# The shifted value copy of a two-layer local attention: fourteen ScalarE activations a batch replaced by DMAs from ScalarE's queue

## The chip, the cores and the metric

The kernel runs on one core of one Trainium2 chip. The metric is the device time of one execution in microseconds; the figure for a kernel is the median of its runs.

## The reference

The program takes 16 sequences ("batches") of 512 tokens with 128 features and runs two residual blocks on each. The first block multiplies a recurrent unit (a log-space gated recurrence, `gru` in the kernel) by a gate that comes from a two-layer transformer with local attention. The second multiplies a global attention (16 heads of 16, softmax over the queries, `glob` in the kernel) by a gate from a mixture of experts. The change lies in the local attention. Windows are of 64 tokens, and a token of window w attends to windows w-1 and w:

```python
bv = v.reshape(b, h, w, WINDOW, d)                 # WINDOW = 64, d = 64, h = 8
def look_around(t):
    p = jnp.pad(t, ((0, 0), (0, 0), (1, 0), (0, 0), (0, 0)))
    return jnp.concatenate([p[:, :, :w], p[:, :, 1:]], axis=3)
bk, bv = (look_around(bk), look_around(bv))
...
out = jnp.einsum('bhwij,bhwjd->bhwid', attn, bv)
```

So each query needs the value rows of its own window and of the one before.

## The kernel before

A batch's 512 tokens are worked on as NT = 4 tiles (t = 0 to 3) of 128 tokens, two windows each. The value rows of tile t lie in `va[:, t]`, tokens on partitions, 8 heads of 64 values and a column of ones (65 floats a head, 520 floats or 2080 bytes in a row for one partition). VectorE writes them out of PSUM (line 1200). The second window of a tile finds the window before it in the upper and lower half of that tile; the first window of a tile needs the last window of the tile before. For that there is a second tensor, `vb`: its lower 64 partitions at tile t hold the lower 64 of `va` at t, and its upper 64 partitions at t + 1 hold the upper 64 of `va` at t. ScalarE fills it, step `("vb", t)`: an activation from partitions 64 to 127 for t = 0, 1, 2 (line 944), and one from partitions 0 to 63 for all four t (line 945). That is 7 activations a layer, 14 a batch and 224 in the program. The reader of `vb` is step `("pv", 2t)` on TensorE (line 725, recorded under the matmul helper's line 587), which first waits for the mark "c" of `("vb", t)` (line 716).

The work of several batches runs at once. Each pass of the outer loop works on lanes: `p` (the projections of local attention: q, k, v, `vb`, the rotation `rot` and `rot2`, the turns `tq` and `tk`, for layer 1 of the batch before and layer 0 of this one), `q` (scores, softmax and its turn, `pturn`), `r` (`pv`, `oturn`, `wo`, and the layer's first feed-forward), `s` (input norm, recurrence, second feed-forward, gate), `g` (the global attention, mostly of two batches back) and `x` (the experts, which run once, in the last pass). The table `ORDER` is a string for each engine which says from which lane the next step comes; each engine issues its instructions in exactly that order, so an instruction that waits holds up everything behind it on its engine. Steps wait for each other by semaphores counted through the tables of marks (`QKV_MARKS` and its like): `need(engine, flow, producer, b, step, mark)` waits until the producer has passed that mark. All DMAs of before are issued from SyncE: the input (line 506), the parts of q and k of the global attention stored to HBM (line 516), their reload in pairs `qs`, `ks` (line 529), and the output (line 534).

Other names in the rows: `e` is the PSUM bank of the projections and of the turns `tq`, `tk` (PSUM out by ScalarE, lines 933 and 957); `scratch<-pb` on line 974 is `pturn` on ScalarE and on line 966 the exponentials of a tile's softmax; `ex` on line 1033 are the exponentials of the global attention, `nmax` on line 1307 their maxima on VectorE; `o_bank` are the global attention's products; lines 889 and 892 are steps of a norm, line 979 is `oturn`.

Of the kernel before, what the change touches and what calls it, by code (L numbers as in the profile page):

```python
# [27 lines left out]
ACT = mybir.ActivationFunctionType  # L28
X = mybir.AxisListType.X

P = 128
B, N, D = 16, 512, 128
NT = N // P
DIN = 256
JG = DIN // P
DEPTH, HEADS, DH, WIN = 2, 8, 64, 64
# [115 lines left out]
def expert_steps():  # L152
# [31 lines left out]
    "q": {"pe": ["p"], "act": ["c"]},  # L184
    "k": {"pe": ["p"], "act": ["c", "sq"]},
    "v": {"pe": ["p"], "dve": ["c"]},
    "vb": {"act": ["c"]},
    "rot": {"dve": ["ss", "max", "c", "s0", "s1"], "pool": ["add"], "act": ["ln", "inv"]},
    "rot2": {"dve": ["n1", "n2", "inv"], "pool": ["q"]},
    "tq": {"pe": ["t"], "act": ["t"]},  # L190
# [71 lines left out]
def lanes():  # L262
# [14 lines left out]


ORDER = {
    "pe": ("3xsgpsxgp8xg4x2gp2xsgxgp28xp4xps2gpspgpxspq3g4xgxpgxqsgqxpsgprpqsp3gpgrqrp3grqxrpgrqr2grpqg2xgxpqgrp"  # L280
           "gqgxprgqpr2gpsgrqprgp3g2r2pgrgpqp2gpqs2grqsgpgpgrpq2gspsgxqpsr2gsrgpqrsprgsgrq2gqgsgprqgpr3gqgrgs2gr"
           "gqsrgq3rsrsrsrgs3r3g4r15g"),
    "act": ("2xsp2gps2gsgp4x2pgs3pg3p2gpxs2g2s2qgqgpg2pqg2pqgp2gpsrg2qgpgq2ps2gxrqgp2qgpgqgspgqpgqrqgpg2pgp2gqp2g"
            "rps2pgpqp3g2qs2gqpspsp2g2pgsgqsgp2qpr2spq3gpgprg2q2gqpsgpsgq3gq2gsr2gq2s2x2qgr4s3r3srs3r17g"),
    "dve": ("xp4x2gs3g2p3x3g17x2s2psps2g2s3gqsgp2sp2gs3xgpxsqg2sr2g2p2grp2grsrgrpq2gsgrp2gr2gqgrspgxp2grgrg2p2gxr"
            "p3grqsgx2psgr2gpgsgsx2gq2gxr3pgrsgrsr3gpqs2g2s2grg2sgr3gqrgs3gr2x2s2rs2r2srsrsrg3s4r9g"),
    "pool": ("gpg2psgs2pgspgs2p2gpg2pgp2g3pgpgsgs3g"),
}


# [33 lines left out]
def need(eng, flow, producer, b, step, mark):  # L324

    if b < 0:
        return
    eng.wait_ge(flow.sem[producer], flow.count(producer, b, step, mark))


def build(nc, a, out):
    ctx = ExitStack()
    with ctx:
        ctx.enter_context(nc.allow_non_contiguous_dma(reason="bias columns, once, a few KB"))

        def sb(name, shape, dt=F32):
            return ctx.enter_context(nc.sbuf_tensor(name, shape, dt))
# [4 lines left out]
        def sem(name):  # L342
            return ctx.enter_context(nc.semaphore(name))
# [4 lines left out]
        qkv = flows["qkv0"], flows["qkv1"]  # L348
# [4 lines left out]
        parts_stored = [sem("parts_even_stored"), sem("parts_odd_stored")]  # L353
        stack_loaded = [sem("stack_even_loaded"), sem("stack_odd_loaded")]
        prep_pe, prep_dve, prep_act, prep_pool = (sem(f"prepared_by_{e}") for e in ("pe", "dve", "act", "pool"))
        expert_loaded = [sem(f"expert_loaded_{i}") for i in range(4)]


# [33 lines left out]
        va, vb = sb("va", [P, NT, HEADS, DH + 1]), sb("vb", [P, NT, HEADS, DH + 1])  # L392
# [192 lines left out]
        def _(pe):  # L585
            def mm(o, l, r, start=True, stop=True):
                return pe.matmul(o, l, r, start=start, stop=stop, skip_group_check=True)  # L587
# [120 lines left out]
            def head_does(l, b, s):  # L708
                f, kind = head[l], s[0]
                if kind == "pv":  # L710
                    u = s[1]
                    t, par = u // 2, u % 2
                    if par:
                        need(pe, f, "dve", b, ("pv", u - 1), "o")
                    else:
                        need(pe, qkv[l], "act", b, ("vb", t), "c")
                        if t:
                            need(pe, f, "dve", b, ("wo", t - 1), "x")
                        elif l == 0:
                            need(pe, head[1], "dve", b - 1, ("wo", NT - 1), "x")  # L720
                    need(pe, attn[l], "act", b, ("pturn", u), "t")
                    for r in range(PAIRS):
                        for w, v in ((0, vb), (1, va)):
                            last = mm(bank_c[WIN * w:WIN * w + WIN, (DH + 1) * r:(DH + 1) * (r + 1)],
                                      probT[u % 2][:, r, WIN * w:WIN * w + WIN], v[:, t, 2 * r + par, :])
                    last.then_inc(f.sem["pe"], 1)
                elif kind == "oturn":
                    t = s[1]
                    need(pe, f, "dve", b, ("pv", 2 * t + 1), "o")
                    for r in range(PAIRS):  # L730
                        last = pe.transpose(bank_c[:, P * r:P * r + P], o_row[:, P * r:P * r + P], ident)  # L731
                    last.then_inc(f.sem["pe"], 1)
                else:
                    t = s[1]
                    need(pe, f, "act", b, ("oturn", t), "t")
                    for r in range(PAIRS):
                        last = mm(bank_c[:, 0:P], wo[:, l, r, :], oT[:, r, :], start=(r == 0), stop=(r == PAIRS - 1))
                    last.then_inc(f.sem["pe"], 1)
# [88 lines left out]
            def expert_does(b, s):  # L827
# [31 lines left out]
                "qkv0": lambda b, s: qkv_does(0, b, s), "qkv1": lambda b, s: qkv_does(1, b, s),  # L859
                "attn0": lambda b, s: attn_does(0, b, s), "attn1": lambda b, s: attn_does(1, b, s),  # L860
                "head0": lambda b, s: head_does(0, b, s), "head1": lambda b, s: head_does(1, b, s),
                "post0": lambda b, s: post_does(0, b, s), "post1": lambda b, s: post_does(1, b, s), "expert": expert_does})


        @block.scalar
        def _(act):
            A = nc.scalar.activation
# [57 lines left out]
            def qkv_does(l, b, s):  # L925
                f, kind = qkv[l], s[0]
                FA = f.sem["act"]
                if kind in ("q", "k"):
                    t, k = s[1], int(kind == "k")
                    if t and kind == "q":  # L930
                        need(act, f, "dve", b, ("rot", t - 1), "s1")
                    need(act, f, "pe", b, s, "p")
                    A(l_qk[:, INNER * k:INNER * (k + 1)], bank_e, ACT.Copy).then_inc(FA, 1)  # L933
                    if k:
                        if t:
                            need(act, f, "pool", b, ("rot", t - 1), "add")
                        need(act, f, "act", b, s, "c")
                        A(l_sq, l_qk, ACT.Square).then_inc(FA, 1)
                elif kind == "vb":

                    t = s[1]
                    need(act, f, "dve", b, ("v", t), "c")
                    if t < NT - 1:
                        A(vb[WIN:P, t + 1, :, 0:DH], va[WIN:P, t, :, 0:DH], ACT.Copy)
                    A(vb[0:WIN, t, :, 0:DH], va[0:WIN, t, :, 0:DH], ACT.Copy).then_inc(FA, 1)
                elif kind == "rot":
                    need(act, f, "dve", b, s, "max")
                    A(stat[:, 16:32], stat[:, 0:16], ACT.Ln, scale=2.0 ** NORM_SHIFT).then_inc(FA, 1)
                    need(act, f, "act", b, s, "ln")
                    A(stat[:, 32:48], stat[:, 16:32], ACT.Exp, scale=-0.5, bias=norm_bias).then_inc(FA, 1)  # L950
                elif kind in ("tq", "tk"):
                    t = s[1]
                    dst = qT[:, :, P * t:P * t + P] if kind == "tq" else kT[:, :, WIN + P * t:WIN + P * t + P]
                    if kind == "tq" and l == 0:
                        need(act, attn[1], "pe", b - 1, ("score", min(t + 1, NT - 1)), "s")
                    need(act, f, "pe", b, s, "t")
                    A(dst, bank_e.rearrange("p (r n) -> p r n", r=PAIRS), ACT.Copy).then_inc(FA, 1)
# [87 lines left out]
            def expert_does(b, s):  # L1045
# [18 lines left out]
            run(act, "act", {  # L1064
                "pre": pre_does, "gru": gru_does, "glob": glob_does,
                "qkv0": lambda b, s: qkv_does(0, b, s), "qkv1": lambda b, s: qkv_does(1, b, s),
                "attn0": lambda b, s: attn_does(0, b, s), "attn1": lambda b, s: attn_does(1, b, s),
                "head0": lambda b, s: head_does(0, b, s), "head1": lambda b, s: head_does(1, b, s),
# [401 lines left out]
```

## Time and profile before

| | us |
|---|---|
| median of 3 runs (lowest, highest) | 3660.54 (3658.41, 3660.62) |
| the profiled execution, whole | 3663.09 |
| its span, first to last instruction | 3661.3 |
| granted TensorE clock, mean | 0.937 |

The span and every row are of the one profiled execution, which lies 2.55 us above the median. Engines are PE (TensorE matmuls), PEld (its weight loads), DVE (VectorE), ACT (ScalarE), POOL (GpSimd) and SP (SyncE). Instructions that wait or that issue a DMA belong to an engine's sequencer (SPq, ACTq) and count as no busy time. The chain of waits is followed back from the last instruction, at each step to what released it or else to the instruction ahead of it on its engine.

### The profile page before, as it was taken

The page shows a single profiled execution, that of the slowest core. Times are in us where ns is not written, and L with a number is a line of the kernel's source. Part 1 is how long each engine was busy: PE and PEld are TensorE (multiplying, and loading weights), DVE is VectorE, ACT ScalarE, POOL GpSimd, SP SyncE. Part 2 cuts the span into 40 slices and gives each one's busy share as a digit, 9 for nine tenths or more (in the row PEclk, how much of TensorE's full clock was granted, in tenths as well). Part 3 has the DMA queues.
Part 4 walks back from the last instruction along what each step waited for, and adds up shares of the span by engine and source line. Part 5 has one row for each costly group of instructions (what it writes and reads, how often), then busy time and mean ns, then how long its engine had stood idle before and what let it go on. Part 6 is the DMA issues. An engine that isn't in the chain of part 4 may idle for free.

```text
span 3661.3 us, 54935 instructions
## 1 busy us (share of the span) xinstructions
PE 3026.1 (83%) x20144; PEld 1454.9 (40%) x20144; DVE 2466.6 (67%) x4573; ACT 2551.7 (70%) x5722; POOL 922.2 (25%) x685
## 2 busy tenths in 40 slices
PE   4677897989888897979889897988889798988776
PEld 2343443434344343524344343534434343433242
DVE  3465867768685877768586776868586776857313
ACT  2466777868686777868677786868677786857444
POOL 1131323223131323313132322323132322312000
PEclk9889998999999999999999999999999998989887
DMA  2001010010101001010101001010101001011200
GB/s 71 3 1 51 18 51 17 14 58 19 58 14 51 21 31 41 14 58 18 54 18 51 21 25 47 14 58 19 54 18 47 21 14 55 19 51 36 83 9 16
DMA packets 113448, 122.78 MB, mean 34 GB/s; under 512 B 13426, under 2 KB 86684, under 8 KB 113180
## 3 DMA queue, kind: packets, MB, share of 16 engines
q1 hardware_dynamic: 113180, 119.26, 10.2%
q8 instruction: 161, 2.64, 0.3%
q14 instruction: 107, 0.88, 0.1%
HBM read 64.70 MB, written 54.53 MB: 33 GB/s over the span
## 4 chain that ended last, share of the span: by engine, by line
PE 45%; DVE 28%; ACT 19%; issue 5%; POOL 2%; SPq 1%; DMA 0%; DVEq 0%; POOLq 0%; ACTq 0%
PE pb L587 19%; PE o_bank L587 11%; PE s L587 6%; DVE nmax L1307 5%; PE e L587 5%; ACT ex L1033 5%; PE e L677 2%; DVE stat L1204 2%; ACT scratch L966 2%; DVE scratch L1213 2%; ACT mlp_h L990 1%; PE pb L731 1%; DVE scratch L1211 1%; DVE scratch L1245 1%; DVE stat L1233 1%
## 5 line engine op out<-in xcount | busy, mean ns | idle before, releaser
L1307 DVE TENSOR_REDUCE nmax<-s 128x1 f32<-128x512 f32 x1024 | 686.6, 684 | 404.1 <-PE s L587 398.3
L1033 ACT ACTIVATE ex<-s,nmax 128x512 f32<-128x512 f32 x1024 | 701.0, 686 | 253.0 <-DVE nmax L1307 218.9
L587 PE MATMUL o_bank<-ex,vsc 128*64 128x512 f32 x2048 | 542.0, 653 | 68.3 <-POOL vsc L1441 53.9
L587 PE MATMUL e<-wqkv,hsh 128*128 128x512 f32 x768 | 432.0, 645 | 85.4 <-ACT scratch L933 68.4
L1402 POOL TENSOR_TENSOR scratch<-scratch 128x1024 f32<-128x1024 f32 x128 | 304.6, 2379 | 768.8 <-DVE scratch L1214 599.7
L587 PE MATMUL s<-qs,ks 96*128 96x512 bf16 x1024 | 387.3, 404 | 121.1 <-ACT ex L1033 112.2
L1441 POOL TENSOR_TENSOR vsc<-vrow,rinv 128x256 f32<-128x256 f32 x256 | 167.6, 655 | 1114.6 <-DVE rinv L1315 770.4
L966 ACT ACTIVATE scratch<-pb,stat 128x128 f32<-128x128 f32 x1024 | 292.3, 375 | 88.6 <-DVE stat L1233 88.6
L1407 POOL TENSOR_TENSOR scratch<-scratch,stat 128x1024 f32<-128x1024 f32 x128 | 243.5, 1902 | 367.5 <-DVE stat L1226 367.5
L587 PEld LDWEIGHTS s<-qs,ks 96*128 96x128 bf16 x1024 | 92.2, 98 | 475.7 <-ACT ex L1033 239.3
L587 PEld LDWEIGHTS o_bank<-ex,vsc 128*64 128x64 f32 x2048 | 135.8, 145 | 341.1 <-issue 233.5
L587 PE MATMUL pb<-vb,scratch 128*64 128x65 f32 (+1 forms) x2176 | 196.5, 236 | 54.4 <-DVE scratch L1245 30.1
L1233 DVE TENSOR_REDUCE stat<-pb 128x4 f32<-128x512 f32 x256 | 164.1, 683 | 105.1 <-PE pb L587 103.8
L705 PE MATMUL pb<-const,scratch 128*128 128x128 f32 x1024 | 167.7, 288 | 70.9 <-ACT scratch L966 70.9
L677 PE MATMUL e<-const,scratch 128*128 128x128 f32 x1024 | 170.6, 292 | 64.7 <-POOL scratch L1407 37.2
L587 PEld LDWEIGHTS pb<-vb,scratch 128*64 128x64 f32 (+1 forms) x2176 | 161.6, 146 | 140.4 <-issue 100.3
L587 PEld LDWEIGHTS e<-wqkv,hsh 128*128 128x128 f32 x768 | 131.6, 196 | 196.0 <-ACT scratch L933 133.5
L587 PE MATMUL pb<-cent,w 128*128 128x512 f32 (+1 forms) x384 | 196.6, 622 | 13.2 <-ACT mlp_h L990 6.0
L1033 ACT ACTIVATION_READ_ACCUMULATOR ex<-s,nmax 128x1 f32 x1024 | 206.0, 201 | 0.0
L933 ACT ACTIVATE scratch<-e 128x512 f32<-128x512 f32 x256 | 152.9, 597 | 69.6 <-PE e L587 58.1
L587 PE MATMUL pb<-va,scratch 128*64 128x65 f32 (+1 forms) x2176 | 197.0, 237 | 0.0
L677 PEld LDWEIGHTS e<-const,scratch 128*128 128x128 f32 x1024 | 126.8, 150 | 147.2 <-issue 73.5
(196 smaller groups left out, 5746.5 us busy)
## 6 DMA issues: line engine op xcount, KB each, us to landing
parts_store<-side SPq DMA_DIRECT2D x64, 384.0 KB, 2.6
qs<-parts_store SPq DMA_DIRECT2D x128, 192.0 KB, 2.7
ks<-parts_store SPq DMA_DIRECT2D x128, 192.0 KB, 3.2
parts_store<-side SPq DMA_DIRECT2D x64, 256.0 KB, 3.0
parts_store<-side SPq DMA_DIRECT2D x64, 128.0 KB, 2.8
xin<-in_L_attn_x SPq DMA_DIRECT2D x16, 256.0 KB, 3.6
out<-o1T SPq DMA_DIRECT2D x16, 256.0 KB, 4.0
wqkv<-in_L_ffn_wqkv SPq DMA_DIRECT2D x1, 1536.0 KB
```

The lines of the kernel that those rows point to most:

```text
L587: return pe.matmul(o, l, r, start=start, stop=stop, skip_group_check=True)
L677: last = pe.transpose(bank_e[:, P * r:P * r + P], l_q[:, INNER * k + P * r:INNER * k + P * r + P], ident)
L705: last = pe.transpose((bank_a, bank_b)[u % 2][:, P * r:P * r + P], prob[u % 2][:, r, :], ident)
L933: A(l_qk[:, INNER * k:INNER * (k + 1)], bank_e, ACT.Copy).then_inc(FA, 1)
L966: last = A(prob[u % 2][:, r, :], sims[:, P * r:P * r + P], ACT.Exp, bias=top[:, r:r + 1])
L1033: A(ex[:, w % 2, j, :], s_bank[c % 2][:], ACT.Exp, bias=nmax[:, c % 8:c % 8 + 1], accum_out=rsum[:, w % 2, j:j + 1]).then_inc(GA, 1)
L1204: V.tensor_reduce(stat[:, 48:64], l_sq.rearrange("p (g d) -> p g d", d=DH), X, ALU.add).then_inc(FV, 1)
L1233: V.tensor_reduce(top, sims, X, ALU.max, negate=True).then_inc(f.sem["dve"], 1)
L1307: V.tensor_reduce(nmax[:, c % 8:c % 8 + 1], s_bank[c % 2][:], X, ALU.max, negate=True).then_inc(GV, 1)
L1402: G.tensor_tensor(l_q, l_c, l_s, ALU.add).then_inc(f.sem["pool"], 1)
L1407: G.tensor_tensor(q, q, stat[:, 96:112].unsqueeze(2).broadcast_to([P, 2 * HEADS, DH]), ALU.mult)\
L1441: G.tensor_tensor(vsc[:, w % 2].rearrange("p (m a) d -> p m a d", a=2), vrow[:, m:m + 2, 2 * V1 * p:2 * V1 * (p + 1)].rearrange("p m (a d) ...
```

## The change

The two activations of step `("vb", t)` become two DMAs issued from ScalarE's queue, from the same rows to the same rows (with the column of ones along). The first waits as before for VectorE's `va`. They count on new semaphores, one for each t, and TensorE's `("pv", 2t)` waits on that one in place of ScalarE's mark. The mark is taken from the table. The four `ORDER` strings are new as well.

```diff
-    "vb": {"act": ["c"]},
+    "vb": {"act": []},
...
+        vb_copied = [sem(f"vb_copied_{t}") for t in range(NT)]
...
-                        need(pe, qkv[l], "act", b, ("vb", t), "c")
+                        pe.wait_ge(vb_copied[t], (2 * b + l + 1) * (32 if t else 16))
...
                     need(act, f, "dve", b, ("v", t), "c")
                     if t < NT - 1:
-                        A(vb[WIN:P, t + 1, :, 0:DH], va[WIN:P, t, :, 0:DH], ACT.Copy)
-                    A(vb[0:WIN, t, :, 0:DH], va[0:WIN, t, :, 0:DH], ACT.Copy).then_inc(FA, 1)
+                        act.dma_start(vb[WIN:P, t + 1], va[WIN:P, t]).then_inc(vb_copied[t + 1], 16)
+                    act.dma_start(vb[0:WIN, t], va[0:WIN, t]).then_inc(vb_copied[t], 16)
```

The new strings hold the same steps, and within a lane the same sequence. What they change between lanes are mostly neighbours that swap places. Among them: on ScalarE, of layer 0, `vb` 2 and `tq` 1 now stand ahead of `pturn` 1 and of the second feed-forward's norm steps (lines 889 and 892), which stood around `vb` 2 before; on TensorE `tk` 1 of layer 0 now stands ahead of a product of the global attention (`av` 10) that stood ahead of it, and `pv` 1 behind the projection `q` 3; the steps of the experts are placed anew between the global attention's in the last pass.

## Rows read from the trace of the kernel before

**Rows 1.** The page: busy time of the engines, and the chain by engine
```profile
PE 3026.1 (83%) x20144; PEld 1454.9 (40%) x20144; DVE 2466.6 (67%) x4573; ACT 2551.7 (70%) x5722; POOL 922.2 (25%) x685
...
PE 45%; DVE 28%; ACT 19%; issue 5%; POOL 2%; SPq 1%; DMA 0%; DVEq 0%; POOLq 0%; ACTq 0%
```

**Rows 2.** Line 898, once a batch, between 1000 and 1700 us: first and last start
```profile
L898 ACT ACTIVATE x_new<-pb x3: 593/593/593, 1190.5 to 1606.9; 128x512 f32<-128x512 f32 x3
```

**Rows 3.** Windows: busy time in one batch's stretch (length, engines, clock, DMA share, GB/s)
```profile
1000.00:1208.20 208.20, 178.88 (x1237) 86.28 (x1236) 152.19 (x281) 156.23 (x355) 57.62 (x43) 0.96 0.10 34
```

**Rows 4.** PE's waits in that stretch (total us, times, longest), those ended by ACT
```profile
PE s L587 <- ACT ex L1033: 5.7, 9, 1.2
PE e L587 <- ACT scratch L933: 3.7, 4, 1.4
PE pb L705 <- ACT scratch L966: 3.7, 4, 2.6
PE e L677 <- ACT qT L957: 1.3, 2, 0.7
```

**Rows 5.** Groups of ACT by line and shape: the copies of the value rows
```profile
L945 ACT ACTIVATE vb<-va 64x512 f32<-64x512 f32 x128 | 80.6, 629 | 1.9 <-DVE va L1200 0.8
L944 ACT ACTIVATE vb<-va 64x512 f32<-64x512 f32 x96 | 60.2, 627 | 39.1 <-DVE va L1200 37.2
```

**Rows 6.** Timeline of ACT: start, us, what, and idle before with releaser
```profile
1002.32 0.60 ACT L957 ACTIVATE qT<-e 128x512 f32<-128x512 f32 x1 [2.06 <-PE e L677]
...
1021.47 0.63 ACT L944 ACTIVATE vb<-va 64x512 f32<-64x512 f32 x1
1022.11 0.63 ACT L945 ACTIVATE vb<-va 64x512 f32<-64x512 f32 x1
1022.64 0.67 ACT L1033 ACTIVATE ex<-s,nmax 128x512 f32<-128x512 f32 x1
...
1026.60 0.60 ACT L957 ACTIVATE kT<-e 128x512 f32<-128x512 f32 x1 [1.86 <-PE e L677]
1027.09 0.59 ACT L974 ACTIVATE scratch<-pb 128x512 f32<-128x512 f32 x1
...
1068.54 0.63 ACT L945 ACTIVATE vb<-va 64x512 f32<-64x512 f32 x1
...
1075.60 0.63 ACT L944 ACTIVATE vb<-va 64x512 f32<-64x512 f32 x1
...
1108.35 0.63 ACT L945 ACTIVATE vb<-va 64x512 f32<-64x512 f32 x1
1108.87 0.59 ACT L979 ACTIVATE scratch<-pb 128x512 f32<-128x512 f32 x1
```

**Rows 7.** The chain in order of time: start, us, what; the copies' place
```profile
1092.94 0.47 ACT scratch L974
...
1093.45 0.63 ACT vb L944
...
1094.09 0.63 ACT vb L945
1094.72 0.57 ACT rstd L889
1095.30 0.49 ACT qT L957
```

**Rows 8.** Timeline of SP's queue: one pair of issues, start and us
```profile
1076.22 0.30 SPq L529 DMA_DIRECT2D qs<-parts_store  x1
1076.56 0.43 SPq L529 DMA_DIRECT2D ks<-parts_store  x1
```

**Rows 9.** SP's issues by tile: ns min/median/max, first and last start; time to landing
```profile
L516 SPq DMA_DIRECT2D parts_store<-side x192: 332/490/1998, 318.2 to 3443.6; - x192
...
DMA to landing us min/median/max: 2.3/2.9/4.7
```

**Rows 10.** Timeline of PE: the first product that reads `vb` of 1068.54
```profile
1090.10 0.24 PE L587 MATMUL pb<-vb,scratch 128*64 128x65 f32 x1 [0.17 <-ACT scratch L974]
```

**Rows 11.** Sequencer instructions that wait on a second semaphore: ns min/median/max
```profile
L328 ACTq EVENT_SEMAPHORE  x789: 17/17/17, 63.2 to 3647.8; - x198
```

More of the change, by code:

```diff
@@ L279 @@
 ORDER = {
[L280 to L287, printed above, removed]
+    "pe": ("7xsg2xpgsp3xg4x2gp2xsgpxg22x2p2xsgxpsp8x2gp4xspgqp3gxqxgsqgr2pspqxsp3gpr3gqrp2grqxrpgrqrgrpq2g2xgpqr"
+           "gpxgqxgprgqpr2gsgprqprgp3grgrpgprpqgpgsgpqrgqspgp2gprgqgsgxpsqsprqgsgrgprsprgsqr3gqgspr2gpqr3gqgrs3g"
+           "rgqsrgq3rsrsrsrgs6r3gr15g"),
+    "act": ("2xsp2gps3g2s2pxpgp3xgx5p2gpg3sqgp2q3gpqpg3pgq2gsrg2qg2pgqpgpsgrqxgp2qgpgqgpsqpgqgqr2g3pgpgq3gsr4p2gp"
+            "qp2g2qs2g2pqp2sgpgpgsgqsgp2qr2sq2p2g2p2grq2gqgqpsgpsgq3gq2gsr2gq2s2qrg4s3r3srs2r2xr17g"),
+    "dve": ("p2gxsg4xgxg2p3x3g7xs3xspxps2xps3x2g2sgqgspg2sgps2g3xpgsq2sr2gpgpxr2gp2grs2rgpq3gsprgr3gqgrsp3xgp2grg"
+            "rpgp2grp3grqsgs2p2grgpgsgsx2gq2grx3pgrsrgsr2gspq3g2sgr2g2sgr3gqgrs3gr2s2rs2r2srsr2xsrg3s4r9g"),
+    "pool": ("gpg2psgspgpspgs2p2gpgpg2p2g3pgpgs4gs"),
 }
```

## The prediction

> **What bounds the kernel now.** I read the busy shares first, then the chain, then one batch's stretch, then the copies themselves. No engine is full: TensorE is busy 83% of the span, ScalarE 70%, VectorE 67%, and the chain that ended last passes through all of them, 45% on TensorE, 28% on VectorE, 19% on ScalarE [rows 1]. A batch takes 208.2 us: line 898 runs once a batch, and three of its starts span 1606.9 - 1190.5 = 416.4 us [rows 2]. In one such stretch TensorE is busy 178.9 us, ScalarE 156.2, VectorE 152.2 [rows 3]. TensorE so idles 208.2 - 178.9 = 29.3 us a batch, and of that 5.7 + 3.7 + 3.7 + 1.3 = 14.4 us (49%) ends with a result of ScalarE [rows 4]. The reader should see a fixed order in which engines hand work to each other: time taken off ScalarE comes back only where somebody waits for ScalarE.
>
> **What is removed.** 128 activations of 629 ns and 96 of 627 ns, 140.8 us busy [rows 5]. Back to back they overlap a little, so their occupancy is read from starts: the pair that starts at 1021.47 lets the next activation start at 1022.64, 1.17 us; the single one at 1108.35 lets it start at 1108.87, 0.52 us [rows 6]. A batch has 6 pairs and 2 singles (t = 3 has no upper half): 6 x 1.17 + 2 x 0.52 = 8.06 us, over 16 batches 129 us, 5% of ScalarE's busy time.
>
> **What is added on ScalarE's queue.** 14 issues a batch, 224 in all. The trace has none on ScalarE; the nearest are SyncE's. One issue takes 0.30 us at best, 0.43 us when it follows another, and a pair 1076.56 + 0.43 - 1076.22 = 0.77 us [rows 8]; the dearest took 1.998 us, a store of parts, one of 192 with a median of 0.49 [rows 9]. I take 0.77 for a pair and 0.43 for a single, since a vb pair too is two short transfers in a row (64 partitions of 2080 bytes each, 133 KB), and keep 0.30 and 2.0 an issue as the ends.
>
> How much of it lies beside other work? An issue is the sequencer's and leaves the engine free to finish the activation ahead of it. The trace has the like: 789 times ScalarE's sequencer takes a second wait between two activations, 17 ns each [rows 11], and one of these stands ahead of the activation of 1027.09 (line 974 has two waits from u = 2 on), which starts 0.49 us after the one ahead, the usual spacing, with no idle time [rows 6]. So I let one activation, 0.5 us, cover an issue: a pair then costs 0.77 - 0.5 = 0.3 us of idle engine and a single nothing. Freed per batch: 6 x (1.17 - 0.3) + 2 x 0.52 = 6.3 us, 100 us over 16 batches. Without any cover it is 6 x (1.17 - 0.77) + 2 x (0.52 - 0.43) = 2.6 us, 41 us; with all issues covered, the whole 129 us.
>
> Queued behind the issue on ScalarE are the turns `tq`, `tk` (line 957), on which TensorE's transposes and scores wait, and the global attention's exponentials (line 1033). The wait for VectorE's `va` is the old one and now stops the sequencer rather than the engine; it ended idle time before the copies for 37.2 + 0.8 us in the whole trace [rows 5], and I put no change there.
>
> On a rule: the Trainium skill (Perfetto Trace Analysis, section DMA Instruction - HWDGE) says that one sequencer at a time has the descriptor generator, and that another waits for the lock. No row shows two queues issuing, but SyncE's pair at 1076.22 falls inside the copies that start at 1075.60 [rows 6, 8]. One such meeting a batch would cost ScalarE up to 0.77 us, 12 us in all; the gain below would be 4 us smaller. I leave it out of the sum.
>
> **What of it reaches the end.** The low end is the chain itself. Of its pieces 32 are copies, 19.4 us together, mostly one pair a batch at the place shown: behind `pturn` (line 974) and ahead of the norm (line 889) and of `tq` (line 957) [rows 7]. That pair is 1.27 us on the chain; with 0.3 us of issue left, it gives 19.4 - 15 x 0.3 = 15 us. At other places the run of activations behind the copies ends in an idle stretch that TensorE ends, as the 2.06 us before 1002.32 and the 1.86 us before 1026.60 [rows 6]: there the copies' time turns into a longer wait for TensorE. The high end for a schedule that answers is the share of TensorE's idle time that ScalarE ends: 49% of 100 us, 49 us. I take the middle, 32 us, 0.32 of what is freed: the copies on the chain go for certain, the rest of ScalarE's lateness only in part, and what is late next is TensorE, which has 29 us of slack a batch at most.
>
> **The new orders.** They keep every step. At the place of [rows 7] two activations that stood between `pturn` and `tq`, or ahead of them, go behind: 0.47 + 0.57 = 1.0 us a batch, 16 us if nothing else were late. The same 16 us is what the moved steps (`pturn` 1, the norm) could cost when they become late. I put 0 and keep 16 both ways. The experts' steps run once, and their new places are of the same kind; they are in the same 16.
>
> **TensorE's wait** on the new semaphores I cost at nothing. The copy of 1068.54 is done at 1069.17 and first read at 1090.10, after a wait for `pturn` (line 974), 20.9 us later, and that is the shortest such distance of the 128 in the trace [rows 6, 10]. A DMA of SyncE landed 2.3 to 4.7 us after its issue [rows 9]. The cover that hides it is the row of rotation, turns, scores and softmax that lies between; it would have to shrink by 16 us before the landing shows. For the same reason the transfers (14 x 133 KB a batch, on DMA engines that are 10% busy [rows 3]) can be slow without harm.
>
> **The sum.** 3663.1 for the profiled execution, less 32, is 3631; the median stands 2.55 us under that execution, so 3660.5 - 32 = 3628.
>
> **Rivals.**
> - The chain moves: other paths are as long as the one shown, and the pair's 15 us are taken up by TensorE's own order or by the moved steps. For it speaks that the copies are 19.4 us of 3661 on the chain, 0.5%. Time 3653 to 3668, no change that can be told.
> - Dear issues, the other side: an issue on ScalarE costs more than on SyncE, because the sequencer that issues is also the one that feeds the engine, so that nothing is started meanwhile. A pair with 0.5 us covered breaks even at 1.17 + 0.5 = 1.67 us, 0.83 an issue. At 1 us an issue a batch loses 6 x (1.5 - 1.17) = 2 us, 32 in all, of which 0.32 reaches the end: 3671. At the dearest row's 2.0 us it is 6 x (3.5 - 1.17) + 2 x (1.5 - 0.52) = 15.9 us, 255 in all, 82 at the end: 3742. For it: no row of an issue on ScalarE. Against it: the median rows are 0.30 to 0.49.
> - ScalarE is the bound: all that is freed comes back, 100 us: 3561. For it: ScalarE runs without a gap around the shown place. Against it: its 52 us of idle time a batch [rows 3]. By the Trainium skill (Advanced Engine Details and Errata, section Sequencer Loop) engine instructions are queued while the sequencer works on another; if that hid every issue, 129 us would be freed and the time by the same 0.32 would be 3619.
> - Nothing covers the issue: it doesn't do all it says. Freed 41 us, 13 at the end: 3647. It lies in the forecast's own case.
>
> **How the numbers follow.** The forecast's own case, 3600 to 3653, has 0.56; all comes back, 0.10; no change, 0.16; slower, 0.18, three quarters of it under 3690. A measurement of this kernel tells about 0.2%, 7 us, from no change. Faster: 0.56 + 0.10 = 0.66. The range reaches from 3585, which takes the forecast's own ends (129 us at 0.49 less 16 of the orders is 3660 - 63 - 16 = 3581) nearly whole, up to 3685, which takes the slower case up to issues of 1.2 us or so; left out are some 0.08 below and 0.07 above.
>
> **What would show it.** Issues on ScalarE's queue of 0.3 to 0.5 us, and an idle engine of about 0.3 us behind a pair. ScalarE's busy time down by 141 us, to 2411. No copy on the chain, and the batch at 206 us instead of 208.2. TensorE's idle time ended by ScalarE under 14.4 us a batch. Landing within 5 us, and no wait of TensorE on it. Wrong would be: issues of over 0.83 us; ScalarE's idle time growing by as much as its busy time falls with the batch still at 208; a wait of TensorE or of SyncE's loads that wasn't there.

## The result and the profile after

| | us, median (lowest, highest, runs) | ratio [95%] |
|---|---|---|
| before, on the same chip | 3660.78 (3656.79, 3663.26, 13) | |
| after | 3670.11 (3666.36, 3676.52, 13) | 1.0029 [1.002, 1.0037] |

The changed kernel is slower, by 9.3 us. The forecast was 3628, faster; the time lies inside the range and on the other side of no change. The profiled execution of after has a span of 3674.3 us. Lines of after stand one lower than those of before (`nmax` on 1308, `qT` on 958).

The page of after, busy time and the chain by engine, against [rows 1]:

```profile
PE 3031.4 (83%) x20144; PEld 1459.6 (40%) x20144; DVE 2480.0 (67%) x4573; ACT 2436.1 (66%) x5498; POOL 918.1 (25%) x685
...
PE 49%; DVE 28%; ACT 12%; issue 5%; POOL 4%; SPq 1%; ACTq 0%; DMA 0%; POOLq 0%; DVEq 0%
```

ScalarE is busy 2551.7 - 2436.1 = 115.6 us less, and its share of the chain falls from 19% to 12%. TensorE's share rises from 45% to 49%: the path that ends last went over to it.

The new issues on ScalarE's queue (ns min/median/max, first and last start), against [rows 8, 9]; under each its time to landing:

```profile
L945 ACTq DMA_DIRECT2D vb<-va x96: 468/468/507, 59.9 to 3332.9; - x96
...
DMA to landing us min/median/max: 2.2/2.2/4.3
```
```profile
L946 ACTq DMA_DIRECT2D vb<-va x128: 467/615/1897, 60.4 to 3359.5; - x128
...
DMA to landing us min/median/max: 2.2/2.4/4.1
```

A pair takes 0.47 + 0.61 us, dearer than SyncE's 0.77. Landing is as quick as forecast, and TensorE's waits name no DMA of `vb`.

Windows of after (columns as in [rows 3]): one pass of 208.4 us and the next, of 212.1.

```profile
1401.20:1609.60 208.40, 178.46 (x1236) 85.82 (x1236) 153.01 (x280) 148.94 (x343) 57.36 (x42) 0.96 0.15 43
1609.60:1821.70 212.10, 182.84 (x1236) 89.18 (x1236) 153.17 (x280) 149.12 (x342) 57.35 (x42) 0.94 0.14 42
```

Before, every pass in the middle of the run takes 208.2 us [rows 2]. After, they go from 208.4 to 212.9 us (start to start of line 899), 210.45 in the mean. The longer of the two passes above has 4.4 us more of busy TensorE for the same 1236 products, at a mean granted clock of 0.94 against 0.96: more of them ran at the lower clock.

Waits of TensorE in the longer pass that ScalarE ends (total us, times, longest), against [rows 4]:

```profile
PE pb L706 <- ACT scratch L967: 5.8, 3, 4.4
PE s L588 <- ACT ex L1034: 5.1, 9, 0.9
PE e L588 <- ACT scratch L934: 3.7, 3, 2.6
PE e L678 <- ACT qT L958: 2.5, 3, 1.3
```

They sum to 17.1 us; it was 14.4. In the pass of 208.4 us the same rows sum to 17.2, so it is the clock and not these waits in which the two passes differ. The turn of q, the last row, has risen from 1.3 to 2.5 us (2.8 in the shorter pass). That row leads to the cause.

### The profile page after: what moved, and what is told of

Read it like the earlier page. It is cut to its first block, busy times and chain, and to the rows that moved or that the text cites. A ratio compares the mean times of both kernels' runs of the same rounds, so it can differ in the third digit from the quotient of the medians.

```text
span 3674.3 us, 54935 instructions
## 1 busy us (share of the span) xinstructions
PE 3031.4 (83%) x20144; PEld 1459.6 (40%) x20144; DVE 2480.0 (67%) x4573; ACT 2436.1 (66%) x5498; POOL 918.1 (25%) x685
## 3 DMA queue, kind: packets, MB, share of 16 engines
q1 hardware_dynamic: 113180, 119.26, 10.1%
## 4 chain that ended last, share of the span: by engine, by line
PE 49%; DVE 28%; ACT 12%; issue 5%; POOL 4%; SPq 1%; ACTq 0%; DMA 0%; POOLq 0%; DVEq 0%
PE pb L588 20%; PE o_bank L588 13%; PE s L588 6%; PE e L588 6%; DVE nmax L1308 5%; DVE stat L1205 3%; PE e L678 2%; ACT ex L1034 2%; DVE scratch L1212 2%; DVE scratch L1214 1%; DVE scratch L1215 1%; PE pb L706 1%; DVE scratch L1246 1%; DVE side L1170 1%; DVE side L1168 1%
## 5 line engine op out<-in xcount | busy, mean ns | idle before, releaser
L588 PE MATMUL e<-wqkv,hsh 128*128 128x512 f32 x768 | 442.9, 660 | 83.6 <-ACT scratch L934 67.5
L588 PE MATMUL s<-qs,ks 96*128 96x512 bf16 x1024 | 395.1, 403 | 114.6 <-ACT ex L1034 103.7
L678 PE MATMUL e<-const,scratch 128*128 128x128 f32 x1024 | 166.5, 287 | 70.4 <-ACT qT L958 42.5
L706 PEld LDWEIGHTS pb<-const,scratch 128*128 128x128 f32 x1024 | 127.3, 150 | 185.7 <-ACT scratch L967 162.0
```

The costliest lines, as they stand in the source:

```text
L678: last = pe.transpose(bank_e[:, P * r:P * r + P], l_q[:, INNER * k + P * r:INNER * k + P * r + P], ident)
L706: last = pe.transpose((bank_a, bank_b)[u % 2][:, P * r:P * r + P], prob[u % 2][:, r, :], ident)
```

## The experiments

The copies changed their means and the four order strings changed with them, so the first four runs take the two apart. In the texts on record, theory K is that TensorE's granted clock takes back what ScalarE gives; theory A, that the freed time has no taker; B, that the DMAs give what was forecast and the new orders lose it; C, that the cost of the issues takes the gain; P, that one place in the new order costs the time; Q, that the new orders cost it as a whole.

**The DMAs or the orders.** `e1` has the DMAs with the order strings of before, `e2` the activations with the new strings. `e3` and `e4` leave the copies out altogether (the shifted rows stay zero), with the old and the new strings; they show what ScalarE's whole freed time is worth. Their edit:

```diff
-    "vb": {"act": ["c"]},
+    "vb": {"act": []},
...
-                        need(pe, qkv[l], "act", b, ("vb", t), "c")
...
-                    need(act, f, "dve", b, ("v", t), "c")
-                    if t < NT - 1:
-                        A(vb[WIN:P, t + 1, :, 0:DH], va[WIN:P, t, :, 0:DH], ACT.Copy)
-                    A(vb[0:WIN, t, :, 0:DH], va[0:WIN, t, :, 0:DH], ACT.Copy).then_inc(FA, 1)
+                    pass
```

> The DMAs of the changed kernel with the four order strings of before. Theory A (no taker): ScalarE's freed time turns into waiting for TensorE and VectorE, whatever the order; this stays within 0.3% of before, 3650 to 3672. Theory B (orders): the copies by DMA give what was forecast and the new orders lose it; then this is at 3615 to 3645. Theory C (issues): what the issues cost ScalarE (in the changed kernel 0.47 and 0.62 us for a pair) takes the gain; then this is at 3655 to 3675 as well, and the kernels without copies tell it from A.

> The activations of before with the four order strings of the changed kernel. Theory A: the orders are worth little with the old load on ScalarE; 3655 to 3690. Theory B: the new orders alone lose 20 to 50 us; 3680 to 3710. Theory C has no say on this one but for the load: the same as before plus the changed kernel's loss, 3665 to 3675.

> The order strings of before; the copies are left out, with TensorE's wait for them (the shifted value rows stay zero). It frees all 129 us of ScalarE and adds no issue. Theory A: 3645 to 3665, the freed time has no taker. Theory B and the forecast's own factor of 0.32: 3610 to 3630. Theory C: far under the kernel with DMAs in the same order, by 25 us or more.

> The order strings of the changed kernel; the copies are left out, with TensorE's wait for them (the shifted value rows stay zero). Theory A: within 10 us of the changed kernel, 3655 to 3675. Theory B: 20 us or more above the kernel without copies in the old order. Theory C: 25 us or more under the changed kernel, 3635 to 3648.

Measured, as us against the kernel before, with the interval of the ratio (3660.16 on that chip; 3660.78 for the DMAs in the new order, which is the kernel after):

| | activations | DMAs | no copies |
|---|---|---|---|
| old order | 0 | -9.1 [0.9964, 0.9985] | -12.8 [0.9951, 0.9976] |
| new order | +37.7 [1.0087, 1.0114] | +9.3 [1.002, 1.0037] | -5.4 [0.9974, 0.9992] |

So the DMAs by themselves do gain, 9 us. Nothing that one does to the copies can gain more than about 13 us in the old order, though 129 us of ScalarE are set free. The new order costs 18 us with DMAs, 38 with activations, 7 with nothing. Of the expectations, `e1` and `e3` came as A had put them and `e2` as B had. `e4` met none: it lies 15 us under the kernel after, where A allowed 10 and C wanted 25, and 7 above `e3`, where B wanted 20. No one of the three theories holds alone: there is little to gain in the old order, and the new one loses by itself, the more, the more ScalarE has to do.

Where the freed time goes shows in ScalarE's own waits (total us, times, longest). Before:

```profile
ACT ex L1033 <- DVE nmax L1307: 218.9, 160, 8.4
ACT scratch L979 <- PE pb L731: 90.8, 65, 4.1
...
ACT qT L957 <- PE e L677: 60.7, 51, 2.5
...
ACT scratch L933 <- DVE scratch L1214: 10.0, 18, 1.8
```

Old order, no copies:

```profile
ACT ex L1030 <- DVE nmax L1304: 249.0, 189, 8.2
ACT qT L954 <- PE e L678: 134.0, 52, 5.8
...
ACT scratch L976 <- PE pb L731: 73.5, 65, 3.7
...
ACT scratch L933 <- DVE scratch L1211: 49.6, 32, 1.8
```

ScalarE comes earlier to the turn of q and waits there 73 us longer for TensorE, 40 us longer for VectorE's rotation (line 1214 of before), 30 us longer for VectorE's maxima, and 17 us less at `oturn`. Smaller rows move too, and the 37.2 us of waiting for `va` ahead of the copies [rows 5] are gone. In all ScalarE is idle for 3647.9 - 2416.2 = 1231.7 us of the span, where it was 3661.3 - 2551.7 = 1109.6: of 135.5 us less busy time 122 became waiting, and 13 came off the span. These are its partners' times, which the copies didn't set: in a middle pass of `e1` the four waits of [rows 4] still come to 5.7 + 3.7 + 3.5 + 0.7 = 13.6 us, where they were 14.4. That pass is 208.2 us, as before; the 10 us of `e1` lie outside the middle passes (three of the first four passes 3.6, 0.4 and 3.0 us shorter, the other 1.2 longer, and 4.7 us at the end).

**Is it the clock?** Two windows of before (columns as in [rows 3]): in the first TensorE mostly waits, 2.6 us of it for the softmax (line 966); in the second, right behind, the granted clock is 0.50, 1.2 GHz.

```profile
1016.00:1019.00 3.00, 1.04 (x6) 0.69 (x6) 2.81 (x5) 2.25 (x7) 0.00 (x0) 1.00 0.00 0
1019.00:1025.80 6.80, 5.29 (x14) 2.42 (x13) 6.42 (x13) 4.97 (x13) 1.90 (x1) 0.50 0.00 0
```

A middle pass of before holds 17.1 us at that level, one of `e1` mostly 23.9, so the clock could have eaten the gain. One pass of `e1` holds 13.7 us, as do two of `e3`, and these take 205.3 us; that pass of `e1` and an ordinary one:

```profile
563.10:768.40 205.30, 177.96 (x1236) 84.81 (x1236) 152.26 (x281) 147.99 (x343) 57.74 (x42) 0.97 0.15 43
1601.20:1809.40 208.20, 181.34 (x1236) 86.69 (x1236) 152.34 (x280) 147.98 (x342) 57.73 (x42) 0.94 0.14 43
```

To see what the freed time is worth with the clock held up, `e5` (as `e1`), `e6` (as before), `e7` (as after) and `e11` (as `e3`, no copies) put 37 products that nobody reads into such waits of TensorE in each pass:

```diff
+            FILL_C = {("glob", ("sim", 3, 1)): 3, ("qkv1", ("k", 1)): 4, ... ("attn1", ("pturn", 0)): 7}
+            FILL_E = {("glob", ("sim", 0, 1)): 1, ("glob", ("sim", 0, 2)): 3, ...}
...
+                        for _ in range(0 if last else table.get((name, tuple(s)), 0)):
+                            mm(dst, identb[:], masks[:, 0, :, :].rearrange("p h n -> p (h n)"))
+                    f(b, s)
```

> The DMAs with the order strings of before, and 37 matmuls a pass (bf16, 128x512, results never read) ahead of waits in which TensorE idled before its granted clock fell. Theory K (the freed time comes back and a lower granted clock takes it): low clock in a pass falls from 23.8 us to under 14, a pass takes 203 to 205.5 us instead of 208.2, and this is 20 us or more under the activations with the same matmuls. Theory A (the freed time has no taker): within 10 us of the activations with the same matmuls.

> The kernel before with the same 37 matmuls a pass. Both theories: the clock stays high for longer here too, a pass of 205 to 208 us, 3610 to 3660 in all. K: 20 us or more above the DMAs with these matmuls; A: within 10 us.

> The changed kernel with the same 37 matmuls a pass at the same steps. K: the passes of 210 to 213 us at a granted clock of 0.936 go, 3620 to 3650. If the new orders lose for reasons of their own (a hand-over that comes late), it stays 15 us or more above the old order with the same matmuls.

> The order of before, the copies of the value rows left out (neither activations nor DMAs, the shifted rows stay zero), and the same 37 products a pass on TensorE whose results nobody reads, so that the clock stays up. Theory A (the freed ScalarE time has no taker in this order): within 10 us of the kernel with activations and these products, 3594 to 3606. Rival K (the clock takes the gain back): 129 us of ScalarE's time are free, and with the clock held up 30 us or more of it come back, 3575 or less.

| with the added products | us, median (range) | ratio [95%] |
|---|---|---|
| `e6`, activations, old order | 3604.06 (3601.51 to 3605.41) | 0.9853 [0.9839, 0.9866] |
| `e5`, DMAs, old order | 3600.68 (3589.12 to 3612.4) | 0.9841 [0.982, 0.9861] |
| `e11`, no copies, old order | 3601.91 (3597.78 to 3607.99) | 0.9845 [0.9832, 0.9858] |
| `e7`, DMAs, new order | 3652.93 (3649.45 to 3658.34) | 0.9988 [0.9979, 0.9996] |

Span and mean granted clock of `e6`, and of `e11`:

```profile
core 0: 3601.2 us, clock 0.963
```
```profile
core 0: 3598.8 us, clock 0.963
```

The products give 53 us to the kernel before (3657.43 on that chip), more than either theory had for `e6`. At the same clock of 0.963 leaving out all copies is worth 3604.06 - 3601.91 = 2 us, 4 when each run is set against before on its own chip, within what the runs scatter. `e5` and `e11` came as theory A had put them. The added products fill waits of TensorE, and could so have taken the room for a gain themselves; but there was room left: in a pass of 204.9 us of `e6` 10.9 us of TensorE's idle time end with ScalarE, in one of 204.6 of `e11` still 10.6. And passes without any time at the lower level take 203.5 us in `e6` and 203.0 in `e11`. So with the clock held up the gain didn't come, and theory A holds there: ScalarE's freed time has no taker. Without the products the passes with the least time at the lower level are the short ones, 205.3 us. The kernel before has no such pass, so whether the clock alone makes them short, and what it takes from the gain there, stays open. `e7` came 3 us above K's range and 52 above `e5`, as its other case had it: the new orders lose for reasons of their own. Why the same products give it only 17 us (14 against before on its own chip) isn't explained; their places were chosen on the old order.

**How dear is an issue?** `e8` splits each DMA of after in two by heads, the same bytes in 28 issues a batch:

```diff
+                    for h in (0, HEADS // 2):
+                        hs = slice(h, h + HEADS // 2)
...
+                            act.dma_start(vb[WIN:P, t + 1, hs], va[WIN:P, t, hs]).then_inc(vb_copied[t + 1], 16)
+                        act.dma_start(vb[0:WIN, t, hs], va[0:WIN, t, hs]).then_inc(vb_copied[t], 16)
```

> The changed kernel with each DMA cut into two by heads: 28 issues a batch instead of 14, the same bytes. If an issue on ScalarE's queue costs what the forecast put (0.5 us covered, the rest idle), four issues take some 2.3 us and leave 1.8 idle where the pair of activations took 1.17; in the new order, where the copies by activation cost 43 us over none, that is some 55 to 70 us over none: 3705 to 3725. If issues are hidden: within 10 us of the changed kernel.

3740.3 us (3737.08 to 3748.73), 1.0223 [1.0207, 1.0239]: 70 us for 224 more issues (74 against before on its own chip), 0.31 us each, half of the 0.6 an issue takes. That is above both expectations. Issues are not all hidden in the new order; TensorE's waits for the turn of q come to 88.9 us in the whole trace, against 42.5 after. Added time on ScalarE costs more in these runs than removed time gives back.

**The place.** On VectorE the maxima of the global attention mark the pass. From the first of `sim` 10 to the first of `sim` 11 (line 1307 of before) it takes 9.9 us in the first fourteen passes of before and of `e1`, 9.8 in `e4`, but 10.5 to 13.4 in after. In that stretch ScalarE's new order has `vb` 1 of layer 0 directly ahead of `tq` 0; before, two of `sim` 9's exponentials and `oturn` stood between. ScalarE and its queue in after (start, us, what, idle before and its releaser):

```profile
1705.46 0.69 ACT L924 ACTIVATE gru_o<-pb,cols 128x512 f32<-128x512 f32 x1
1705.98 0.47 ACTq L945 DMA_DIRECT2D vb<-va  x1
1706.03 0.60 ACT L980 ACTIVATE scratch<-pb 128x512 f32<-128x512 f32 x1
1706.49 0.61 ACTq L946 DMA_DIRECT2D vb<-va  x1
1707.20 0.60 ACT L958 ACTIVATE qT<-e 128x512 f32<-128x512 f32 x1 [0.57 <-issue]
```

and TensorE in the same stretch:

```profile
1707.86 1.11 PE L678 MATMUL e<-const,scratch 128*128 128x128 f32 x4 [1.26 <-ACT qT L958]
1708.76 1.91 PE L588 MATMUL pb<-scratch,wo 128*128 128x128 f32 x8
1710.47 0.99 PE L588 MATMUL e<-wqkv,hsh 128*128 128x512 f32 x1
```

The two issues take 1.1 us, the one activation behind which they run (line 980) covers half, and the turn of q starts 0.57 us late. TensorE has waited 1.26 us, and the products behind it are slow: eight of `wo` take 1.91 us.

It isn't so at every place. Layer 1's `vb` 2 in the same pass of after: four exponentials of the softmax (line 967) and one of the global attention (line 1034) stand ahead of it in ScalarE's string, and they start only while the issues run or after them:

```profile
1643.55 0.61 ACT L920 ACTIVATE side<-side 128x512 f32<-128x512 f32 x1
1643.56 0.47 ACTq L945 DMA_DIRECT2D vb<-va  x1
1644.07 0.61 ACTq L946 DMA_DIRECT2D vb<-va  x1
1644.07 1.12 ACT L967 ACTIVATE scratch<-pb,stat 128x128 f32<-128x128 f32 x4
1645.07 0.70 ACT L1034 ACTIVATE ex<-s,nmax 128x512 f32<-128x512 f32 x1
```

ScalarE is not idle in this stretch. Of the eight `vb` steps in a pass of after five stand directly ahead of a turn; where ScalarE is idle ahead of the others, it waits for TensorE's product anyhow. The idle time of ScalarE that ends with an issue, in the whole trace of after (total us, times, longest), is that of one place:

```profile
ACT qT L958 <- issue: 10.3, 14, 1.9
```

`e9` moves that one step of after back ahead of `sim` 9 2, past two exponentials, the recurrence's last step and `oturn`; `e10` moves it, in `e1`, behind to `tq` 0. Their edits in ScalarE's string, and that of `e12`, which gives after the whole ScalarE string of before:

```diff
 e9, in the string of after
-    ... qgqr2g3pgpgq3gsr4p2gp ...
+    ... qgqr2g3pgpgqgp2gsr3p2gp ...
 e10, in the string of before
-    ... 2pgp2gqp2grps2pgpqp3g ...
+    ... 2pgp2gq2gr2ps2pgpqp3g ...
```

> The changed kernel with one step moved: on ScalarE, `vb` 1 of layer 0 stands three places earlier, ahead of the global attention's `sim` 9 2 as in the order of before, and no longer directly ahead of `tq` 0. Theory P (the place costs the time: the two issues hold up the turn of q, TensorE waits for it, its clock falls and VectorE gets the next scores late): the step from `sim` 10 0 to `sim` 11 0 on VectorE goes from about 12 us back to 9.9 in most passes, the pass from 210.4 to about 208.4, and the time from 3670 to 3652 to 3660. Rival Q (the new orders as a whole cost it, the place is only where it shows): the time stays within 3665 to 3675.

> DMAs in the order of before, with only that one step moved the other way: `vb` 1 of layer 0 stands directly ahead of `tq` 0 on ScalarE, as in the new order. Theory P: the time goes up from 3651 by 8 to 20 us, to 3659 to 3671, with the step from `sim` 10 0 to `sim` 11 0 above 10.5 us. Rival Q: within 5 us of 3651, the step at 9.9.

> The changed kernel with ScalarE's order string of before; the strings of TensorE, VectorE and GpSimd stay the new ones. If the loss of the new orders sits in ScalarE's string: 3648 to 3656, as the DMAs with all strings of before (3651). If it sits in the other engines' strings: 3662 to 3675.

| | us, median (range) | ratio [95%] | `sim` 10 to 11, middle passes |
|---|---|---|---|
| after | 3670.11 (3666.36 to 3676.52) | 1.0029 [1.002, 1.0037] | 10.5 to 13.4 |
| `e9`, step moved back | 3651.91 (3647.47 to 3657.7) | 0.9981 [0.9972, 0.999] | 9.8 (one 10.1) |
| `e1` | 3651.02 (3645.89 to 3655.96) | 0.9974 [0.9964, 0.9985] | 9.9 |
| `e10`, step moved behind | 3674.43 (3672.55 to 3679.69) | 1.0043 [1.0029, 1.0057] | 10.6 to 12.4 |

Against the kernel before on its own chip (3659.58 for `e9` and `e10`) after is at +9.3 and `e9` at -7.7, `e1` at -9.1 and `e10` at +14.9: one step is worth 17 us in the new order and 24 us in the old one. Theory P holds, Q falls: `e9` lies 0.1 us under the range that P gave it and `e10` 3.4 above. In `e10` the place itself takes 1.25 us a pass more than in `e1`, and the pass grows by 2.2 (208.18 to 210.39); the rest lies elsewhere in the pass. TensorE's waits for the turn of q come to 30.5 us in the whole trace of `e9`, as in `e4` without copies, and 42.5 after. `e9` in the same stretch; ScalarE and its queue, then TensorE:

```profile
1694.61 0.69 ACT L1033 ACTIVATE ex<-s,nmax 128x512 f32<-128x512 f32 x1 [0.31 <-DVE nmax L1307]
1694.61 0.47 ACTq L944 DMA_DIRECT2D vb<-va  x1
1695.12 0.61 ACTq L945 DMA_DIRECT2D vb<-va  x1
1695.19 0.19 ACT L1033 ACTIVATION_READ_ACCUMULATOR ex<-s,nmax 128x1 f32 x1
1696.13 0.69 ACT L1033 ACTIVATE ex<-s,nmax 128x512 f32<-128x512 f32 x1 [0.74 <-DVE nmax L1307]
...
1698.51 0.61 ACT L957 ACTIVATE qT<-e 128x512 f32<-128x512 f32 x1
```
```profile
1699.18 0.66 PE L677 MATMUL e<-const,scratch 128*128 128x128 f32 x4 [0.57 <-ACT qT L957]
1699.67 1.06 PE L587 MATMUL pb<-scratch,wo 128*128 128x128 f32 x8
```

The same issues now run out while ScalarE waits for VectorE's maxima anyhow. They cost nothing there (no idle time of ScalarE in all of `e9` ends with an issue), TensorE's wait is 0.57 us, and the eight products take 1.06. The windows show the clock beside it, of after and of `e9`:

```profile
1706.00:1722.00 16.00, 13.76 (x112) 7.99 (x110) 10.68 (x23) 10.87 (x29) 4.82 (x3) 0.89 0.10 25
```
```profile
1698.00:1714.00 16.00, 13.87 (x120) 7.67 (x119) 12.94 (x27) 12.47 (x32) 5.45 (x4) 1.00 0.10 26
```

The loss has two parts. The wait is 1.26 - 0.57 = 0.69 us longer, and in passes of after in which the clock stays up `sim` 10 to 11 takes just that much more, 10.49 against 9.80. In seven of the first fourteen passes the clock falls as the products behind the wait begin, and the distance is 11.95 us or more: the slow products cost about 1.5 us on top. The mean excess of the fourteen is 1.65 us: 0.7 of it the wait, 0.15 two issues that took longer than usual (below), 0.8 the slow products. A pass is 210.45 - 208.92 = 1.5 us longer than in `e9`, some 20 us in the 13 middle passes; the runs measured 17, and the profiled execution of after lies 6 us above its median. By whole passes the clock's part is the larger one: of the 13 the six in which it falls there take 211.8 us in the mean, the other seven 209.3. Why it falls in one pass and not in the next isn't shown.

By the Trainium skill (TensorE: Matmul & The Clock Gate, section HAM oscillation — how this bites in real kernels) waits that come back between short runs of products bring the clock down each time, so that a wait costs more than its length. The trace agrees in half of the passes: 0.7 us more of wait, and where the clock fell, 1.5 us more of slow products.

`e12` missed both expectations, with 3815.54 us (3813.71 to 3818.3), 1.0428 [1.0414, 1.0442]. Its waits of TensorE, and those of after:

```profile
PE pb L706 <- ACT scratch L967: 167.6, 84, 8.0
PE s L588 <- ACT ex L1034: 134.0, 186, 1.9
```
```profile
PE pb L706 <- ACT scratch L967: 103.8, 56, 8.0
PE s L588 <- ACT ex L1034: 103.7, 163, 1.9
```

A string of one order among three of the other makes TensorE wait 94 us longer at two lines alone. The strings belong together, and one of them can't be judged by such an exchange; a single step can. That the new strings cost 38 us with activations was not followed further; two activations in the same place are part of it (10 to 11 takes 11.1 to 13.9 us in `e2`).

The quickest kernels are those with the added products, 3600.68 with the DMAs and 3604.06 with the activations: the products bring the gain, and the DMAs add nothing that these runs can tell.

## Why the prediction was wrong

**What is removed**, 129 us of occupancy, was measured by no run by itself. The busy time fell by 116 us to 2436, not by 141 to 2411; without any copy it is 2416.2 in the old order and 2429.2 in the new one, since the 141 counted overlapped time twice.

**The issues** were priced the same everywhere, and they differ by place. A pair takes 1.08 us, not 0.77, and at `tq` 0, where one activation covers 0.5 us as assumed, 0.57 us stay open, not 0.3. In the rest of the trace less is open than forecast: 10.3 us end with an issue, all at that place, and some 18 with 15 pairs ahead of `rot` that leave 0.54 us and that the profile puts to VectorE. The forecast had 96 x 0.3 = 29 us. The Trainium skill's rule (Advanced Engine Details and Errata, section Sequencer Loop) that would have hidden every issue agrees with the pair of 1643.56 and does not fit the 0.57 us at `tq` 0. So not less ScalarE time was freed than forecast, but the part that was lost stood where TensorE waits. An issue of 0.54 us in the mean of a pair is under the break-even of 0.83; the rival of dear issues did not happen as it was priced.

**What reaches the end** was the first step that failed. The factor of 0.32 should have been 0.10: leaving out all 129 us gains 13, and the DMAs in the old order gain 9. The low end, 15 us from the chain's own copies, came near in size by luck: it was to come from one pair in each batch, and the pass of `e1` stayed at 208.2, with its gain in the first passes and at the end. The share of TensorE's idle time that ScalarE ends says who came last, not how far ahead the next one was: without the copies 122 of ScalarE's 135.5 us less busy time became waits of its own, and with the DMAs in the old order 13.6 of the 14.4 us that TensorE waited for it in a pass remained.

**The new orders** put at 0 was the step that failed in sign. They cost 18 us with the DMAs, just over the 16 that were kept, and nearly all of it is one step. The prediction saw `vb` 2 and `tq` 1 move, and not that `vb` 1 came to stand directly ahead of `tq` 0; it named the danger for that kind of place (the turns queued behind the issue) and priced it at 0.3 us a pair, without asking for each of the eight steps what stands behind it and would have been ready. The clock's share, 0.8 of 1.65 us at that place, stood in no term.

**TensorE's wait on the new semaphores** was right: no wait on a DMA of `vb`, landing 4.3 us at most, 20.9 us of cover before [rows 10] and 21.1 after.

**The rivals.** The chain moves, 3653 to 3668, is what the change would have been in the old order or with the step moved back (3651 to 3652, a little better). The slower side came by a mechanism that had been given no case of its own.

**The lock of the descriptor generator** that was left out of the sum is not shown. Two issues of 224 were long, 1.40 and 1.90 us, each in the costly place. SyncE's pair had ended 1.87 us ahead of both, as it had ahead of that place's issues of ordinary length in the other passes. In `e1` three were long, with SyncE's last issue 10 to 18 us away. What lengthens them is open; the Trainium skill (Perfetto Trace Analysis, section DMA Instruction — HWDGE) would have it a wait for another queue's issue, and no row here bears that out.

## What to carry to other kernels

Time taken off an engine that hands work back and forth is worth what its partner has waited for it beyond the next thing that is late; leave the work out for a run, and that ceiling is measured before anything is built. An instruction moved to a queue is priced by its place: list for each what stands directly behind it, whether that would have been ready, and who waits for it, and put it ahead of a wait that the engine has anyhow. In a fixed order look at single steps that moved ahead of a hand-over, since one of them can cost twice what the whole change gains.

## What was not expected of the hardware

- An issue on ScalarE's queue took 0.47 us as the first of a pair and 0.61 as the second, SyncE's 0.30 and 0.43 [rows 8]; ten of the 896 in the traces of after, `e1`, `e9` and `e10` took 0.8 to 1.9.
- An issue can run while activations that stand ahead of it in the order have yet to start: the pair of 1643.56 was out at 1644.68, and an exponential ahead of it started at 1645.07. At 1705.98 one activation was left to cover the pair, and 0.57 us stayed open.
- 37 products a pass that nobody reads shortened the kernel before by 53 us, 1.5%, by holding the granted clock up (0.963 in the mean, 0.937 before).
